# The first 32 samples of a cross-network prepared tile by tile

## The reference

```python
def _cin_layer(X0, Xi, W, b):          # Wr: [128, 39, Fi]
    return jnp.einsum('hjk,bjd,bkd->bhd', Wr, X0, Xi) + b[None, :, None]
X0 = Xi = e                            # [512, 39, 16]
for W, b in ((W0, b0), (W1, b1), (W2, b2)):
    Xi = _cin_layer(X0, Xi, W, b)      # [512, 128, 16]
    res.append(Xi.sum(axis=2))
h = jnp.concatenate([*res, dense_ctx], axis=1)             # [512, 400]
h = jnp.maximum(h @ W_top1 + b_top1, 0)                    # 512
h = jnp.maximum(h @ W_top2 + b_top2, 0)                    # 256
y = h @ W_top3                                             # 1
```

## Time and profile before

| | |
|---|---|
| Median of 3 runs | 696.32 us (695.7 to 696.78) |
| The profiled execution's own time | 697.1 us |
| Its span, first to last instruction | 695.2 us |
| TensorE matmuls busy | 651.2 us, 94% |
| TensorE weight loads busy | 495.7 us, 71% |
| VectorE busy | 566.9 us, 82% |
| ScalarE busy | 410.4 us, 59% |
| GpSimd busy | 444.2 us, 64% |
| Chain that ended last, by engine | PE 88%, POOL 4%, DVE 3%, DMA 2% |
| Mean granted TensorE clock | 0.993 |

### The profile page before, as it was taken

One profiled execution on the slowest core, in us unless ns is written; L12 is line 12 of the kernel. 1 busy time (PEld: TensorE's weight loads), 2 busy tenths in 40 slices (PEclk: granted clock), 3 DMA queues, 4 the chain that ended last, 5 costly groups with the idle time before them and its releaser, 6 DMA issues.

```text
span 695.2 us, 10601 instructions
## 1 busy us (share of the span) xinstructions
PE 651.2 (94%) x2856; PEld 495.7 (71%) x2856; DVE 566.9 (82%) x1495; ACT 410.4 (59%) x1369; POOL 444.2 (64%) x372
## 2 busy tenths in 40 slices
PE   0079999999999999999999999999999999999997
PEld 0046777777778777777778877777778777777767
DVE  4039999999994599999995589999997479999980
ACT  3025767666663466767673476767674366767751
POOL 6746777777783377777775367777775366454440
PEclk9999999999999999999999999999999999999999
DMA  6246424040403103122221201313030300300000
GB/s 214 49 128 232 151 60 122 6 124 6 124 7 105 24 3 88 43 64 68 58 75 42 83 7 37 95 28 103 18 114 17 99 16 18 111 1 6 0 2 1
DMA packets 39055, 44.33 MB, mean 64 GB/s; under 512 B 17427, under 2 KB 22253, under 8 KB 38867
## 3 DMA queue, kind: packets, MB, share of 16 engines
q1 hardware_dynamic: 33363, 42.34, 20.0%
q0 software_dynamic: 5632, 1.31, 2.1%
HBM read 8.86 MB, written 0.00 MB: 13 GB/s over the span
## 4 chain that ended last, share of the span: by engine, by line
PE 88%; POOL 4%; DVE 3%; DMA 2%; issue 2%; SPq 1%; ACT 1%; POOLq 0%; DVEq 0%
PE p_u L541 20%; PE p_u L542 20%; PE p_u L543 20%; PE p_x L518 13%; PE p_tower L560 5%; PE p_g L551 5%; POOL emb L257 3%; DVE parts L449 1%; DVE x2t L457 1%; PE p_tower L587 1%; PE p_tower L573 1%; DMA emb<-table_in,idx_all 1%; PE p_tower L572 1%; PE p_tower L579 1%; PE p_x L508 1%
## 5 line engine op out<-in xcount | busy, mean ns | idle before, releaser
L331 ACT ACTIVATE prod<-p_u,x0t 128x128 f32<-128x128 f32 x1024 | 290.9, 369 | 140.4 <-PE p_u L543 140.1
L449 DVE SCALAR_TENSOR_TENSOR parts<-p_u,x0t,parts 128x128 f32<-128x128 f32 x1024 | 283.7, 343 | 50.4 <-PE p_u L543 50.3
L541 PE MATMUL p_u<-w1h,x1h 128*128 128x512 f32 (+1 forms) x640 | 303.9, 475 | 4.1 <-DVE x1l L426 2.3
L542 PE MATMUL p_u<-w1l,x1h 128*128 128x512 f32 (+1 forms) x640 | 250.4, 391 | 0.0
L543 PE MATMUL p_u<-w1h,x1l 128*128 128x512 f32 (+1 forms) x640 | 250.2, 391 | 0.0
L273 POOL TENSOR_TENSOR parts<-parts,prod 128x512 f32<-128x512 f32 x128 | 173.1, 1353 | 77.6 <-ACT prod L331 66.3
L257 POOL DMA_INDIRECT emb<-table_in,idx_all x176 | 181.3, 1030 | 51.2 <-issue 47.8
L541 PEld LDWEIGHTS p_u<-w1h,x1h 128*128 128x128 f32 x640 | 120.9, 189 | 52.6 <-issue 20.4
L268 POOL TENSOR_TENSOR parts<-prod 128x512 f32<-128x512 f32 x64 | 89.6, 1400 | 99.6 <-ACT prod L331 99.3
L542 PEld LDWEIGHTS p_u<-w1l,x1h 128*128 128x128 f32 x640 | 121.5, 190 | 42.8 <-issue 20.2
L543 PEld LDWEIGHTS p_u<-w1h,x1l 128*128 128x128 f32 x640 | 120.7, 189 | 25.8
(11 more groups left out here) (46 smaller groups left out, 204.6 us busy)
## 6 DMA issues: line engine op xcount, KB each, us to landing
fac_b<-xx SPq DMA_DIRECT2D x96, 234.0 KB
fac_a<-xx SPq DMA_DIRECT2D x48, 78.0 KB
emb<-table_in,idx_all POOLq DMA_INDIRECT x176, 2.5
g_all<-w_in SPq DMA_DIRECT2D x3, 832.0 KB, 9.8
xx<-xx SPq DMA_DIRECT2D x32, 78.0 KB
fac_b<-xx SPq DMA_DIRECT2D x16, 156.0 KB
w<-w_in SPq DMA_DIRECT2D x1, 2496.0 KB, 10.3
bd<-x0t SPq DMA_DIRECT2D x128, 10.0 KB, 2.1
```

The source lines that it names most:

```text
L331: last = nc.scalar.activation(dst[:, i * H:(i + 1) * H], u[:, i * H:(i + 1) * H], ACT.Copy, scale=x0t[:, par, t, j:j + 1])
L449: nc.vector.scalar_tensor_tensor(out=chain[:, p, i, :], in0=u[:, i * H:(i + 1) * H], scalar=x0t[:, par, t, j:j + 1], in1=add, op0=ALU.mult ...
L541: nc.tensor.matmul(u, xh, wh, start=True, stop=False)
L542: nc.tensor.matmul(u, xh, wl, start=False, stop=False)
```

## The change

Macro 0 is prepared one tile at a time, from the gathers as they land. Its samples are taken in the order in which the gathers bring them (`FIRST_PARTS`: 3, 3, 2 and 3 gathers for its four tiles). For each tile TensorE picks its columns out of `emb` with a slice of an identity matrix (`first_x0_rows`), makes the factors fac_a and fac_b, shifted copies of those rows, by eight matmuls with 0/1 matrices `rep_a` and `rep` (`first_factors`, into the banks p_x1, p_g and p_tower), and transposes. ACT takes the rows, fac_a and x0t out; DVE multiplies straight from PSUM (`first_products`). Layer 0 of the tile is seven matmuls of 128 columns. Tile 0 is prepared ahead of the loop, tile t + 1 in the slots of tile t. Macro 1's products and layer 0 move to slots 30 to 39, the last tile of macro 0. `eye` grows to 117 x 117 (zeroed by DVE, filled by ACT's queue), `rep` is loaded there too. W1's three parts are issued after the first three gathers have landed, last part first, and the quads run from j = 35 down. The gathers get a quota for each tile: 4, 4, 4, 4, 4, 4, 3, 3, then 3, 3, 3, 2. The context's and the output's first 32 columns are reordered (three strided DMAs, three more copies by ACT). The counts of semaphores follow. In ACT's loop `first_columns`, `first_factor`, `first_x0t` and `first_x1` of tile t + 1 stand at slots 1, 4, 5 and 9 of tile t, each ahead of that slot's `scale_quad`. `place_first_bd(t, ...)` is `place_bd` for tiles t and t + 1: eight DMAs.

```diff
@@ constants
-G_BATCH = [range(8, GATHERS), range(0, 3), range(3, 6), range(6, 8)]
-G_AHEAD = [2, 3, 3, 3]
+FIRST_PARTS = [range(0, 3), range(3, 6), range(6, 8), range(8, GATHERS)]
+F_X0, F_X0_OUT, F_PICK, F_PICK_OUT, F_XT_OUT, F_LAYER0, F_X1 = 0, 1, 3, 4, 5, 8, 9
+F_S_COLUMNS, F_S_XT = 31, 32
+F_S_PAIR = [30, 31, 32, 34, 35, 36, 37]
+F_S_ADD = [33, 34, 35, 36, 37, 38, 39]
+F_S_X1, F_S_Z1 = 39, 31
+GATHER_ORDER = [(M, g) for M in range(2, MACROS * BLOCKS) for g in range(GATHERS)]
+GATHER_QUOTA = [4] * 4 + [4, 4, 3, 3] + [3, 3, 3, 2] * (MACROS * BLOCKS - 2)
-QUAD_J = [list(range(36, 39))] + [list(range(4 * q, 4 * q + 4)) for q in range(9)]
+QUAD_J = [list(range(36, 39))] + [list(range(4 * q, 4 * q + 4)) for q in reversed(range(9))]
@@ sync, ahead of the loop
-            spread(0, 0, first=True)
+            sp.wait_ge(first_in[0], 16 * len(FIRST_PARTS[0]))
             step = F * H // W1_PARTS
             for i in range(W1_PARTS):
+                c = slice((W1_PARTS - 1 - i) * step, (W1_PARTS - i) * step)
+                sp.dma_start(w1_raw[:, c], w1_d[:, c]).then_inc(w1_in[i], 16)
+            sp.wait_ge(bd_cleared, 1)
+            sp.wait_ge(f_xt_made, 2)
+            place_first_bd(0, f_bd_in)
             spread(1, 1)
-            sp.wait_ge(x0t_made, 1)
-            sp.wait_ge(bd_cleared, 1)
-            place_bd(0)
+            sp.wait_ge(f_xt_made, TILES)
+            place_first_bd(2, bd_in[0])
             sp.dma_start(w2[:].rearrange("k j h -> k (j h)"), w2_d).then_inc(w2_in, 16)
...
-            sp.dma_start(ctxt[:], ctx_d).then_inc(tower_in, 16)
+            for c in range(STACK):
+                n, at = FIRST_SAMPLES[c], GATHERS * c
+                sp.dma_start(ctxt[:, c:MACRO_B:STACK], ctx_d[:, at:at + n], allow_slow_non_contiguous=True).then_inc(tower_in, 16)
+            sp.dma_start(ctxt[:, MACRO_B:B], ctx_d[:, MACRO_B:B]).then_inc(tower_in, 16)
@@ scalar, ahead of the loop
+            first_columns(0)
+            first_factor(0)
+            first_x0t(0)
+            high_half(0)
+            high_half(1)
+            first_x1(0)
+            high_half(2)
@@ scalar
+            def first_x1(t):
+                c = slice(t * 128, (t + 1) * 128)
+                act.wait_ge(f_l0_full, t + 1)
+                nc.scalar.activation(x1f[:, c], p_x1[:, c], ACT.Identity, bias=b0).then_inc(f_x1f_made, 1)
+                act.wait_ge(f_x1f_made, t + 1)
+                nc.scalar.activation(x1h[:, 0, c], x1f[:, c], ACT.Copy).then_inc(f_x1h_made, 1)
@@ vector, in the loop and ahead of it
+                        if M == 0 and 0 < tt and q == 0:
+                            first_x1l(tt)
+                        if M == 0 and tt < TILES - 1 and q == F_XT_OUT:
+                            first_products(tt + 1)
...
                         if q % 2 == 1:
                             chain_quad(T, tt, q)
+                        if M == 0 and s == F_S_X1:
+                            make_x1l(M + 1, (m + 1) % 2)
...
+            first_products(0)
+            low_half(0)
+            first_x1l(0)
+            low_half(1)
+            low_half(2)
@@ tensor
+            def first_x0_rows(t):
+                for i in range(t + 1):
+                    pe.wait_ge(first_in[i], 16 * len(FIRST_PARTS[i]))
+                need(pe, f_x1f_made, t)
+                o = p_x1[0:F, t * 128:(t + 1) * 128].rearrange("p (s d) -> p s d", d=D)
+                for c in range(STACK):
...
+                    last = nc.tensor.matmul(o[:, s0:TILE_B:STACK, :], eye[0:(c + 1) * F, c * F:(c + 1) * F],
+                                            emb[0:(c + 1) * F, 0, g0 * D:g1 * D].rearrange("p (g d) -> p g d", d=D),
+                                            start=True, stop=True)
+            def first_factors(t):
+                x0 = first_x0[:, t * 128:(t + 1) * 128]
+                pe.wait_ge(f_x0_made, t + 1)
+                need(pe, f_z_made, 2 * t)
+                nc.tensor.matmul(p_x1[0:ROWS, t * 128:(t + 1) * 128], rep_a[:], x0,
+                                 start=True, stop=True).then_inc(f_a_full, 1)
+                for k in range(GROUPS):
+                    o = p_g[0:ROWS, k * 128:(k + 1) * 128] if k < 4 else p_tower[0:ROWS, (k - 4) * 128:(k - 3) * 128]
+                    last = nc.tensor.matmul(o, rep[:, k:k + ROWS], x0, start=True, stop=True)
...
+                pe.wait_ge(f_a_made, t + 1)
+                nc.tensor.transpose(p_x1[:, t * 128:t * 128 + F], x0, eye[0:F, 0:F]).then_inc(f_xt_full, 1)
@@ tensor, layer2
                 pe.wait_ge(x2_made, T + 1)
-                pe.wait_ge(bd_in[par], 16 * TILE_B * (pair + 1))
+                if T < 2:
+                    pe.wait_ge(f_bd_in, 16 * TILE_B)
+                    pe.wait_ge(f_z_made, 2 * TILES)
+                else:
+                    pe.wait_ge(bd_in[par], 16 * TILE_B * (pair + 1))
@@ tensor, in the loop
+                        if M == 0 and q == 0:
+                            pe.wait_ge(f_x1h_made, tt + 1)
+                            pe.wait_ge(f_x1l_made, tt + 1)
+                        if M == 0 and tt < TILES - 1:
+                            if q == F_X0:
+                                first_x0_rows(tt + 1)
+                            if q == F_PICK:
+                                first_factors(tt + 1)
+                            if q == F_LAYER0:
+                                first_layer0(tt + 1)
```

More of the change, by code:

```diff
@@ L204, in spread, with place_first_bd @@
                     sp.dma_start(fac_a[i * F:(i + 1) * F, par, :], xx[row:row + F, par, :]).then_inc(a_in[par], 16)
-                if first:
+                if M == 1:
                     sp.wait_ge(w0_summed, 1)
                 for k in range(GROUPS):
-                    need(sp, z0_made, GROUPS * (M - 1) + k + 1)
+                    need(sp, z0_made, GROUPS * (M - 2) + k + 1 if M > 1 else 0)
                     sp.dma_start(fac_b[0:GROUP_ROWS[k], k, :], xx[k:k + GROUP_ROWS[k], par, :]).then_inc(b_in[k], 16)
+            def place_first_bd(t, done):
+                for b in range(TILE_B):
+                    sp.dma_start(bd[b * D:(b + 1) * D, 0, t:t + 2, b, :], x0t[b * D:(b + 1) * D, 0, t:t + 2, :]
+                                 ).then_inc(done, 16)
             def place_bd(par):
@@ L254, in _, with gather @@
         def _(pool):
-            def gather(M, g):
+            def gather(M, g, landed):
                 rows, e, at = GATHER_ROWS[g], M % EMBS, GATHERS * M + g
@@ L274, in body @@
                                                 op=ALU.add).then_inc(summed, 1)
[L275 to L281, removed]
-            pool.wait_ge(idx_made, 1)
[L284 to L288, removed]
+                    at = sum(GATHER_QUOTA[:T])
+                    for M, g in GATHER_ORDER[at:at + GATHER_QUOTA[T]]:
+                        if g == 0 and M == EMBS:
+                            pool.wait_ge(f_x0_full, TILES)
+                        elif g == 0:
+                            need(pool, x0_in, 16 * STACK * (M - EMBS))
+                        gather(M, g, gathered[M % EMBS])
+            pool.wait_ge(idx_made, 1)
+            for t in range(TILES):
+                for g in FIRST_PARTS[t]:
+                    gather(0, g, first_in[t])
+            for g in range(GATHERS):
+                gather(1, g, gathered[1])
             over_blocks(body)
@@ L413, in _, with first_products, first_x1l @@
         def _(dve):
+            def first_products(t):
+                c = slice(t * 128, (t + 1) * 128)
+                dve.wait_ge(f_a_made, t + 1)
+                need(dve, f_l0_full, t)
+                for bank, ks in ((p_g, range(0, 4)), (p_tower, range(4, GROUPS))):
+                    n = len(ks)
+                    dve.wait_ge(f_b_full, 2 * t + (2 if ks[0] else 1))
+                    nc.vector.tensor_tensor(out=first_z0[:, ks[0]:ks[0] + n, :],
+                                            in0=bank[0:ROWS, 0:n * 128].rearrange("p (k c) -> p k c", c=128),
+                                            in1=fac_a[:, 0:1, c].to_broadcast([ROWS, n, 128]),
+                                            op=ALU.mult).then_inc(f_z_made, 1)
+            def first_x1l(t):
+                c = slice(t * 128, (t + 1) * 128)
+                dve.wait_ge(f_x1h_made, t + 1)
+                nc.vector.tensor_tensor(out=x1l[:, 0, c], in0=x1f[:, c], in1=x1h[:, 0, c].bitcast(FP32),
+                                        op=ALU.subtract).then_inc(f_x1l_made, 1)
             def product(M, pair, par, k):
                 rows = GROUP_ROWS[k]
-                dve.wait_ge(a_in[par], 16 * STACK * (pair + 1))
-                dve.wait_ge(b_in[k], 16 * (M + 1))
-                need(dve, l0_added, GROUPS * M + max(k - Z_RING + 1, 0))
+                dve.wait_ge(a_in[par], 16 * STACK * (pair + par))
+                dve.wait_ge(b_in[k], 16 * M)
+                if M == 1:
+                    dve.wait_ge(f_l0_full, TILES)
+                need(dve, l0_added, GROUPS * (M - 1) + max(k - Z_RING + 1, 0))
```

(9 more changed lines are left out.)

198 lines of the change are left out of this document (138 added, 60 removed).

## The result

The changed kernel took 700.18 us (median of 20 runs, 696.53 to 704.98), the kernel before 696.51 beside it (20 runs, 694.65 to 698.08): a ratio of 1.0058, 95% interval 1.0036 to 1.0080. It is slower by 3.7 us, and its times are spread over 8.5 us where those of before lie within 3.4. The profiled execution took 701.5, span 699.6 against 695.2.

The account below looks back on a forecast made before the run. TensorE was taken to bound the kernel past 85 us. Late macro 2 copies gave +0.3 at quad 6 of tile 4, half clock +1.6: +1.9 on the median 696.3, hence 698.2 us; range 693.0 to 702.5.

Parts of the forecast that it names:

- The likeliest case: Whole kernel: macro 2's late copies use up the earlier start, half clock follows; 697.2 to 699.5 us, chance 0.33.
- rival D: Tiles 0 to 2: thin matmuls bring half-clock spells, or ACT or DVE is slower than counted; 699.5 to 702.5 us, chance 0.20.
- the +1.9: Total loss forecast: +0.3 us at quad 6 of tile 4 plus +1.6 of half clock after its wait.
- Start, 19.8: TensorE's first `p_u` matmul, forecast at 19.8 us, 27.3 earlier than before.
- T0 to T1, 33.6 and 46.7: Tiles 0 and 1 forecast to take 13.8 and 13.1 us, so tile 1 starts at 33.6, tile 2 at 46.7.
- Border waits, 1.9: At each of four tile borders TensorE waits for the next tile's x1, 1.9 us.
- Layer 2's wait in T2, 2.6: In tile 2, slot 4, TensorE idles 2.6 us until DVE makes tile 0's last `f_z_made` at slot 5.
- half clock in T2: After tile 2's idle of 2.6, half clock slows layer 2 and quad 4: 0.4 us taken, 0 to 1.2.
- The copies' chain, 24.2: From issue of the weights to macro 2's products, 24.2 us as before: weights from 63.2, products ready at 88.3.
- The strided loads: Three `ctxt` loads ahead of `xx<-emb` in SP's queue: 0.5 us taken, between nothing and 2.8.
- Quad 6 of T4, 90.1, and then 1.6 of half clock: TensorE begins that quad at 90.1 to 90.2, against 89.93, after some 4 us idle; half clock then costs 1.6.
- What is late next: macro 2's copies: Their products, ready at 88.3 us, hold TensorE at quad 6 of tile 4, ending the 6.7 us lead at its start.

Follow-up runs that it names:

- e3: Changed kernel plus filler matmuls (results overwritten) at the first macro's four borders and ahead of tile 0's layer 2: 707.18 us, 1.0103 of the kernel before.
- e1: Changed kernel with the loads of w2, tower weights and context issued after macro 2's copies: 707.33 us, 1.0107 of the kernel before.
- e4: Changed kernel with macro 2's transposes, products and layer 0 three slots later within macro 1: 708.81 us, 1.0146 of the kernel before.
- e5: Changed kernel with macro 2's row and factor copies issued ahead of the weights, gather quotas adapted: 709.33 us, 1.0112 of the kernel before.
- e7: The changed kernel unaltered, run again as control on the second chip: 708.32 us, 1.0133 of the kernel before.
- e9: Changed kernel with macro 1's eleven gathers issued after tile 0's sums: 705.95 us, 1.0117 of the kernel before.
- e2: Changed kernel with layer 2 of tile 0 and the copy after it moved from slot 4 to slot 7: 703.17 us, 1.0040 of the kernel before.
- e6: Changed kernel with macro 2's copies ahead of the weights, tile 0's layer 2 at slot 7, six fillers per border: 700.29 us, 0.9988 of the kernel before.
- e12: e6 plus sixteen fillers around the start of tile 0 and macro 3's gathers one tile sooner: 689.81 us, 0.9884 of the kernel before.
- e10: e6 with macro 1's eleven gathers issued after tile 0: 697.62 us, 1.0018 of the kernel before.

## Why the prediction came out as it did

The forecast was 698.2 with slower as the likeliest sign; measured 700.2, slower by 0.58%. The likeliest case (697.2 to 699.5) wasn't it: rival D (699.5 to 702.5) was, half-clock spells within T0 to T2. That the sign came out as forecast is in part luck: the +1.9 was 0.3 of wait for the copies at quad 6 and 1.6 of half clock behind a long wait there, and neither happened so; the loss arose earlier, in T2 and T3.

- **Start, 19.8.** Right: 19.89.
- **T0 to T1, 33.6 and 46.7.** 32.33 and 46.37. T0 was 12.9 and not 13.8, since in that execution the clock had risen by 18.5; I had counted 1.5 for half clock. Without that the count was too low: at full clock the matmuls of T0 and T1 took 11.3 each and not 10.6, so that T1 took 14.0 and not 13.1, and the two errors nearly cancel. In other executions T0's matmuls took 1.6 to 6.0 us more. That this depends on the execution I hadn't seen.
- **Border waits, 1.9.** Right: 1.61, 2.06, 1.86, and one of 2.77 where DVE's x1l took 1.33.
- **Layer 2's wait in T2, 2.6.** Right: 2.37 (2.6 on the other chips).
- **The term that was mis-sized: half clock in T2, "0.4 taken (0 to 1.2)".** T2 took 22.9 us and not 15.7. The clock fell at 45.8, in the border wait of 2.77, and stayed at 0.50 for 17.1 us; e3 with fillers made the same tile in 16.7. The size belongs to that execution: in e1, e4, e5, e7 and e9, with 3.4 to 6.8 us of half clock at that place, T2 took 18.2 to 19.1, still over the forecast. I had taken the spell behind the 2.26 us of idle in the earlier trace rows, 3.4 us long, as the size of every spell. Before, TensorE had full quads behind it; in T2 there were further gaps (layer 2's wait) and thin matmuls, and which of them made the spell so long isn't shown. T3 lost 1.9 more (17.6 for 15.7).
- **Rival D's mechanism** was half right. It put the spells on the thin matmuls; e2, e3, e6 and e12 have all of these, and no fall in T2. There, filling the gaps or moving one was enough. But the thin matmuls have a share elsewhere: in e12 the clock fell at 14.1, when TensorE had run little but 39-row matmuls from 10.77 on, with gaps of 0.54 and 0.34 only. And not every gap brings a fall (e2 has two border waits of 2.06 between 43.4 and 84.4). No run takes the thin matmuls away and leaves the gaps. The row that it leaned on, 16-row matmuls before half clock at 229, doesn't repeat in every execution either: e12 has the same matmuls at 220 to 223 and no fall.
- **The copies' chain, 24.2.** Right: 24.1. The strided loads, 0.5 in the sum, took 5.38 us of SyncE's queue and delayed nothing, by a margin of 1.75. That it hangs on x0t of tile 3 was right too: weights at 67.9 and not 63.2, since T2 was slow; product at 92.0 and not 88.3.
- **Quad 6 of T4, 90.1, and then 1.6 of half clock.** 93.81, and the half clock lay ahead of it (86.8 to 90.2) and not behind, as no wait of 4 us came. In sum +3.9 here and +4.3 at T8, where I had +1.9.
- **"What is late next: macro 2's copies".** Only half of it: they bound if T4 is early (e3, e10: 3.6 and 3.9 us of wait at quad 6). In the changed kernel TensorE's own T2 and T3 bound as well, and mending the copies alone gave nothing (e1, e5).

## What to carry to other kernels

An earlier start is worth only what is left of it at the first point where the old schedule was already dense; here 27 us shrank to less than nothing on the way, in gaps of 2 us and in half clock around them. When work is put on TensorE in small pieces with waits between, price the tile at both clock levels, and look for what fills the gaps: 40 fillers that compute nothing, one wait moved three slots and another order of copies and gathers went from 3.7 us lost on one chip to 8 won on another. A kernel whose times spread more than its neighbour's is telling something: look at several executions before you explain one.

## What the runs showed of the hardware that I had not expected

- The time of the clock's first rise isn't set by the program alone: 18.5, 24 to 25, or 32 to 33 us, with TensorE's first matmul at 9.1 to 10.2 each time. The three latest rises belong to the three earliest first matmuls (9.12 to 9.30), the two earliest to 9.48 and 9.62, the six between to 9.38 to 10.21: too few to make a rule of. The Trainium skill, "TensorE: Matmul & The Clock Gate", section "What's actually happening", also says that the number of slow matmuls at a kernel's start differs from run to run; these traces agree.
- The clock column tells nothing before its first reading: layer 0 of tile 0 took 0.24 an instruction at 15 us, and that of tile 1, in T0, 0.12, both under 1.00. The durations of equal matmuls tell the clock.
- On one chip TensorE's increments came up to 8 us after its matmuls (e5: 39.06 for a quad done, as recorded, by 30.85), in six profiles several within 0.3 us. On that chip a trace keeps 8,858 to 9,190 semaphore updates, on the others 11,798 to 11,870, and of the landings of macro 1's gathers before 40 us 36 to 80 of 176. Records were lost in the same traces in which increments were late, but also in e2's (9,078 kept), where they weren't. The Trainium skill, "NOTIFIC — the notification-queue block", section "7.1 Overflow: three behaviours, one of which stalls the engine", says that a full queue of records, in one of its settings, stalls its producer; no run here shows whether that is what happened, or whether it would without a trace. The cause stays open.
